# A decoder block on one core: the stores of empty slot rows and the place of the first residual sum

## The reference

```
x = layernorm(x + attn(x))                       # 16 heads of 16, rotary, no mask
x = layernorm(x + xattn(x, ctx, mask) @ Wo.T + bo)
x = layernorm(x + moe(x))                        # 8 experts, top 2, 256 -> 1024 -> 256, gelu
```

## Time and profile before

| | |
|---|---|
| profiled execution | 2272.11 us |
| its span, first to last instruction | 2270.4 us |
| median of three runs | 2275.64 us (2265.1 to 2276.37) |
| TensorE busy | 2163.7 us (95% of the span) |
| VectorE, ScalarE, GpSimd busy | 1200.3, 1004.9, 601.0 us |
| mean granted TensorE clock | 0.965 |

### The profile page before, as it was taken

One profiled execution on the slowest core, in us unless ns is written; L12 is line 12 of the kernel. 1 busy time (PEld: TensorE's weight loads), 2 busy tenths in 40 slices (PEclk: granted clock), 3 DMA queues, 4 the chain that ended last, 5 costly groups with the idle time before them and its releaser, 6 DMA issues. The chain is left out here.

```text
span 2270.4 us, 48602 instructions
## 1 busy us (share of the span) xinstructions
PE 2163.7 (95%) x18846; PEld 1506.0 (66%) x18846; DVE 1200.3 (53%) x2522; ACT 1004.9 (44%) x1538; POOL 601.0 (26%) x937
## 2 busy tenths in 40 slices
PE   7899999999999999999999999999799999999990
PEld 4566666666666666666666666666478778787780
DVE  3466676766767767777677776764111111111114
ACT  1355555555555555555555555553231222212225
POOL 2113222332223322233222332222212122121223
PEclk6899999999999999999999999998799999999995
DMA  6311111211101110011000010000113332333217
GB/s 179 105 29 31 35 31 49 65 36 62 34 27 36 37 30 24 22 28 34 28 25 23 27 34 24 27 20 13 37 35 84 77 68 36 82 84 77 24 17 303
DMA packets 97666, 115.72 MB, mean 51 GB/s; under 512 B 12096, under 2 KB 91021, under 8 KB 95392
## 3 DMA queue, kind: packets, MB, share of 16 engines
q1 hardware_dynamic: 68112, 82.38, 11.7%
q0 software_dynamic: 17664, 18.35, 5.2%
q10 hardware_dynamic: 11664, 11.88, 1.8%
HBM read 64.53 MB, written 56.05 MB: 53 GB/s over the span
## 5 line engine op out<-in xcount | busy, mean ns | idle before, releaser
L867 DVE TENSOR_REDUCE smax<-ps_s 128x4 f32<-128x1024 f32 x500 | 609.3, 1219 | 311.3 <-PE ps_s L574 265.8
L753 ACT ACTIVATE prob<-ps_e 128x1024 f32<-128x1024 f32 x500 | 511.9, 1024 | 525.6 <-PE ps_e L583 403.6
L574 PE MATMUL ps_s<-stack 17*128 17x256 f32 x4000 | 573.7, 404 | 26.6 <-DVE smax L867 21.1
L583 PE MATMUL ps_e<-stack 18*128 18x256 f32 x4000 | 572.4, 404 | 6.9 <-DMA stack<-nrows 5.1
L574 PEld LDWEIGHTS ps_s<-stack 17*128 17x128 f32 x4000 | 347.8, 186 | 207.8 <-issue 115.8
L583 PEld LDWEIGHTS ps_e<-stack 18*128 18x128 f32 x4000 | 344.6, 186 | 12.2 <-DMA stack<-nrows 7.1
L1534 ACT ACTIVATE hid<-m_ps_h,b_sb 128x320 f32<-128x320 f32 x256 | 135.0, 527 | 415.5 <-PE m_ps_h L1494 415.5
L1494 PE MATMUL m_ps_h<-m_cols,w_sb 128*128 128x320 f32 x1024 | 293.1, 435 | 0.6 <-DVE m_cols L1551 0.6
L1511 PE MATMUL m_ps_o<-w_sb,hid 128*128 128x256 f32 x1280 | 278.9, 379 | 0.0
L1511 PEld LDWEIGHTS m_ps_o<-w_sb,hid 128*128 128x128 f32 x1280 | 243.2, 190 | 34.8
L599 PE MATMUL ps_w<-prob,val 128*32 128x256 f32 x4096 | 257.5, 394 | 1.7 <-ACT prob L753 1.7
(11 more groups left out here) (134 smaller groups left out, 2241.8 us busy)
## 6 DMA issues: line engine op xcount, KB each, us to landing
w_sb<-in_w SPq DMA_DIRECT2D x16, 1024.0 KB, 6.4
slot_rows_dram<-fill ACTq DMA_DIRECT2D x8, 1290.0 KB, 10.7
m_rows<-slot_rows_dram SPq DMA_DIRECT2D x16, 645.0 KB, 4.7
xT<-in_xT SPq DMA_DIRECT2D x32, 256.0 KB, 2.8
ctxT<-in_ctxT SPq DMA_DIRECT2D x32, 256.0 KB, 2.8
x_res<-in_x SPq DMA_DIRECT2D x32, 256.0 KB, 3.1
stack<-nrows SPq DMA_DIRECT2D x512, 2.0 KB
sums_dram<-x SPq DMA_DIRECT2D x32, 256.0 KB, 2.2
```

The costliest lines, as they stand in the source:

```text
L574: mm = nc.tensor.matmul(scores[:, p % 2, t, :], stack[X][rows, Q, p // HG, t * P:(t + 1) * P], stack[X][rows, K, p // HG, :], start=True, ...
L583: mm = nc.tensor.matmul(shifted[:, p % 2, t, :], stack[Y][rows, K, h // HG, t * P:(t + 1) * P], stack[Y][rows, Q, h // HG, :], start=True, ...
L753: nc.scalar.activation(prob[:, h:h + 2, :].rearrange("p h s -> p (h s)"), shifted[:, :, :, :].rearrange("p h t s -> p (h t s)"), ACT.Exp, ...
L867: nc.vector.tensor_reduce(max_columns(X, p), scores[:, :, :, :], AX.X, ALU.max)\
```

## The change

Two edits. On ScalarE the nine transfers of empty rows are asked for at other duos: n and a rest are taken from (2i + X - 2) * 8 + m divided by 3, and a transfer is issued where the rest is 0. They are thus issued at m = 0, 3, 6 of the self step of i = 1, m = 1, 4, 7 of its cross step, m = 2, 5 of the self step of i = 2, and m = 0 of its cross step. On VectorE the two residual additions of the first layer norm are issued at p = 3 of the self step, directly behind the division, with their two waits (x loaded, division done); the statistics stay at p = 5.

```diff
             def emit(i, X, Y, bX, bY):
                 a = at[X]
                 for m in range(DUOS):
-                    n = (2 * i + X - 1) * DUOS + m
-                    if 0 <= n <= E:
+                    n, rest = divmod((2 * i + X - 2) * DUOS + m, 3)
+                    if 0 <= n <= E and rest == 0:
                         empty_rows(n)
...
-            def first_norm(b):
+            def first_sum(b):
                 dve.wait_ge(res_in.sem, res_in.count(b))
                 dve.wait_ge(ln[SELF].sem, ln[SELF].count(b, 4))
                 for t in range(T2):
                     nc.vector.tensor_tensor(y[:, t, :], att[:, t, :], x_res[:, t, :], ALU.add).then_inc(ln[SELF].sem, 1)
-                mean_and_variance(SELF, b, 6, y, stats)
...
                         if there(bX - 1) and p == 3:
                             divide(SELF, bX - 1, 0)
                             divide(SELF, bX - 1, 1)
+                            first_sum(bX - 1)
                         if there(bX - 1) and p == 5:
-                            first_norm(bX - 1)
+                            mean_and_variance(SELF, bX - 1, 6, y, stats)
```

## The result

The changed kernel takes 2276.04 us (median of 20 runs, 2270.17 to 2284.53), the kernel before, in runs taken side by side with these, 2272.61 us (20 runs, 2263.61 to 2276.77). The ratio is 1.0024 [1.0013, 1.0036]: by that the change costs 5.4 us (the bare medians are 3.4 apart). It is inside the range and inside the 0.5% called no change, but on the slower side by more than its interval. The profiled execution took 2278.57 us (span 2276.8) against 2272.11 (span 2270.4).

The account below looks back on a forecast made before the run. TensorE was taken to bound the attention part, so only its waits cost time. First edit -7.3 + 3.7 = -3.6 us, second +5.1, sum +1.5 on the profiled 2272.1: 2273.6, given as 2274; range 2260 to 2285.

Parts of the forecast that it names:

- What goes in the first edit: First cross step: TensorE's 4.38 us wait, 0.22 at 34.99 and the slow matmuls behind go; -7.3 us.
- What comes in the first edit: Self steps of i = 1 and 2: new waits for small transfers beside moved large ones, +3.7 us.
- the third place: Self step of i = 2, m = 5: small transfers partly overlapped by a large one, a wait of 0.6 us.
- Rival D: Start: the clock falls anyway, 4.6 us go, new waits cost 5.3 and low-clock stretches 6.8; +12.6 us, 2285; 12%.
- The second edit: Self steps: fourth duo waits 0.58 us, the fifth's 0.41 wait goes; +0.17 us a step, 30 times, +5.1 us.
- A: Self steps: the sums fit in, fourth duo doesn't wait and the fifth no longer waits; -15.9 us, 2256; 12%.
- B: Start: small transfers aren't late beside a single large one, so no new waits; -2.2 us, 2270; 14%.
- C: Self steps: fourth reduction stays late, so both fourth and fifth duo wait; +13.8 us, 2286; 10%.
- The sum: Whole kernel: -3.6 + 5.1 = +1.5 us on the profiled 2272.1 gives 2273.6; 2274 was given.
- The rule weighed: DMA engines go round queues packet by packet: small transfers equally late, 11.9 us, however many large ones; new waits 7.3, 6.1, 6.4.

Follow-up runs that it names:

- e3_transfers_apart: The changed kernel's transfers with three moved away from small transfers with near deadlines, sums as before, against the kernel before: 2263.62 us, ratio 0.997.
- e2_sums_only: Only the two additions moved behind the division, transfers as before, against the kernel before: 2278.06 us, ratio 1.0036.
- e4_merge_late: Only the merging of the statistics moved from p = 5 to p = 7, against the kernel before: 2263.97 us, ratio 0.9975.
- e6c_one_sum_each: One of the two additions moved behind the division, the other left at p = 5, against the kernel before: 2269.43 us in one run, before 2269.19.
- e7c_sums_early_merge_late: Both additions moved behind the division and the merging to p = 7, against the kernel before: 2280.08 us in one run, before 2269.19.
- e1_transfers_only: Only the empty rows' transfers moved as in the change, sums as before, against the kernel before: 2272.65 us against 2270.6, ratio 1.0007.
- e8_one_beside: e3_transfers_apart with the sixth transfer back at m = 2 of the self step of i = 2, against the kernel before: 2435.98 against 2438.67 us, 0.999.

## Why the forecast time was near and its working wrong in one half

- **What goes in the first edit: right.** -7.3 us worked out, -7.7 in the profile at the next step; TensorE, no longer standing still at 46.34, kept its clock.
- **What comes in the first edit: the step that failed.** It took 3.7 us of waits and nothing behind them. The waits were 1.93 (2.1 forecast), 2.17 (1.0), 0.34 where none was forecast, and none at the third place (0.6): 4.4 together, not far off in sum. The second wait was under-sized mostly because the small transfers took 121.57 - 113.90 = 7.7 us from their first issue, not 6.8; TensorE also came 0.3 us earlier than worked out (119.40 - 113.90 = 5.5 us behind that issue, not 5.8). At the third place the large transfer was issued 3.5 us ahead of the small ones (128.28 and 131.79), whose four issues then took 2.42 us, as with none beside them. What the sum left out was the slow stretch behind a wait: 3.2 us behind 121.57 (12.4 - 9.2), and behind 80.56 between 2.1 (the lead lost up to 108.48 less the wait there, 2.4 - 0.3) and 2.9 (the windows). So this term was 3.7 and is 4.4 + 5.3 = 9.7 by the duos. The prediction had just read this for the wait that it removed, 2.7 of the 7.3 us, and did not charge it to the waits that it added. Rival D did, at 3.4 us each, and was given 12%; in its mechanism it is what happened, though the 7.3 were gained in full, which D denied. Not every slow stretch hangs on a collision, as `e3_transfers_apart` shows, so the sizes of a single profile are rough.
- **The second edit: right in its mechanism, under-sized.** New wait 0.58 forecast, 0.57 to 0.58 measured at the fourth duo; the old one gone. But the fourth duo comes 0.64 us later, since the sums start 0.11 behind the division and not 0.04, and so a round is +0.22 instead of +0.17. In the profile the rounds' stretch grows by 4.9 us where 5.1 were forecast (6.2 in `e2_sums_only`); that these two meet is luck, from the end of the attention part. `e4_merge_late`, `e6c_one_sum_each` and `e7c_sums_early_merge_late` show the reason given: no slack ahead of the third reduction, 0.41 us too much ahead of the fourth.
- **Rivals A, B and C** fell. A wanted rounds of 47.0, and they are 47.65. B wanted no wait for small transfers behind 60 us, and there are three. C wanted a late fourth reduction, and it waits 0.25 us for the scores.
- **The sum.** +1.5 forecast, +5.4 [3.0, 8.2] measured. The first edit is +1.6 instead of -3.6 by its own ratio, the second +8.2 [4.1, 12.3] against +5.1; they add to 9.8, more than the change shows, within the intervals. The time came within 2 us of the forecast (2276.0 against 2274) by luck. The forecast mixed two bases: it put +1.5 on the profiled execution (2272.1) and set the result beside a median 3 us above that of the 20 runs. So the number was near, while the change it stood for was a gain of 1.6 us and not a loss.
- **The rule weighed** (the Trainium skill, "DMA: Bandwidth & Descriptors", "Queues, rings and completion order") would have had 11.9 us for each small transfer beside a large one. The rows here have 80.56 - 73.92 = 6.6, 7.7 in the change, 7.7 and 7.9 in `e1_transfers_only`, 7.3 in `e8_one_beside`: beside one large transfer it is not 11.9, and the wait removed did not come back in each place. The rows go against it as the whole story.

## What to carry to other kernels

A wait of TensorE is priced with what stands behind it: where one removed gives back its slow stretch, one added takes one, here 1.0 to 3.2 us for waits of 1.9 to 3.0 (the 1.0 is `e1_transfers_only` behind 85.07). Moving a large transfer paid here only where no small one with a near deadline was issued beside it, so lay out the small ones' issue times first. To shorten a block of VectorE that ends late, move out what nobody needs soon (the merging) rather than move work ahead of a reduction that the next engine already waits for.

## What the hardware showed beyond that

How long ScalarE's queue takes to issue one of these transfers, and how long the transfer takes to land, depend on how many are under way. These are L729's lines after; before they were 366/498/1006 ns and 6.5/10.7/13.3 us:
```profile
L729 ACTq DMA_DIRECT2D slot_rows_dram<-fill x8: 366/367/382, 53.8 to 128.3; - x8
...
DMA to landing us min/median/max: 5.8/6.0/6.9
```
And a single large one stretches the issue of small ones on another engine's queue if both are issued together. In SP's rows after, the first and second stand within 0.3 us of a large one (73.64 and 114.13), the third 3.5 us behind one (128.28), and it takes no longer than with none.
```profile
73.92 3.90 SPq L439 DMA_DIRECT2D stack<-nrows  x4
...
113.90 3.20 SPq L439 DMA_DIRECT2D stack<-nrows  x4
...
131.79 2.42 SPq L439 DMA_DIRECT2D stack<-nrows  x4
```
Two of the four chips on which the experiments ran slowed every kernel, before's to 2438.67 and 2443.08 us where it takes 2269 to 2273 on the others: in nearly every round VectorE and ScalarE stop for 2 to 4 us behind the scatters and TensorE waits for them about 3, and the trace names something outside the core ("remote"). The waits of VectorE (160 to 1500 us) and the timeline of `e6_one_sum_each`, and a window of it:
```profile
DVE smax L867 <- remote: 61.8, 24, 3.0
```
```profile
706.21 1.23 DVE L867 TENSOR_REDUCE smax<-ps_s 128x4 f32<-128x1024 f32 x1 [2.74 <-remote]
...
707.48 0.48 PE L574 MATMUL ps_s<-stack 17*128 17x256 f32 x2 [3.07 <-DVE smax L867]
```
```profile
704.00:708.00 4.00, 0.93 (x10) 0.52 (x13) 1.76 (x3) 1.50 (x2) 0.94 (x1) 1.00 0.32 106
```
TensorE is busy 0.93 of 4 us at a granted clock of 1.00. Its cause stays open: kernels of the same code had no such stall on the other two chips, and nothing was tried that takes it away.
